# One clip instruction per attention step on VectorE, fed by four score matmuls in a row on TensorE, and a one-matmul output bias

## The reference

```
scores = einsum('bhnd,bhjcd->bhnjc', q, kc) / sqrt(Dh)
scores = clip(scores, -10.0, 10.0)
scores = where(mask == 0, -10.0, scores)
attn = softmax(scores, axis=-1)                 # over the 128 keys of one chunk
ctx = einsum('bhnjc,bhjcd->bhnd', attn, vc)
out = layernorm(ctx @ Wo.T + bo + x_normed) * gamma + beta
```

## Time and profile before

| | |
|---|---|
| median of 3 runs | 833.86 us (832.61 to 836.44) |
| profiled execution | 836.42 us, span 834.6 us, mean granted PE clock 0.904 |
| PE busy | 700.5 us, 84% |
| DVE busy | 727.4 us, 87% |
| ACT busy | 567.0 us, 68% |
| POOL busy | 556.9 us, 67% |
| chain that ended last | PE 43%, DVE 31%, POOL 12%, issue 10% |
| first clip to end of last clip | 38.58 to 513.39 us |

### The profile page before, as it was taken

The page is one execution under the profiler, slowest core; times in us unless marked ns, Lnnn a source line. Parts: engine busy times, 40 slices in busy tenths (PEclk is TensorE's granted clock), DMA queues, the critical chain, the costliest instruction groups (busy, mean ns, idle before and its releaser), DMA issues.

```text
span 834.6 us, 20579 instructions
## 1 busy us (share of the span) xinstructions
PE 700.5 (84%) x6443; PEld 366.1 (44%) x6443; DVE 727.4 (87%) x2032; ACT 567.0 (68%) x1091; POOL 556.9 (67%) x570
## 2 busy tenths in 40 slices
PE   4598699999999999999999898575620499999994
PEld 1322133333323233233333123464510499999994
DVE  4989999999999999999999999987661288888883
ACT  4596587897897987978978666534500377777772
POOL 1211557897887897987978999868777155555554
PEclk9789899999999999999999999555555599999998
DMA  8924503204105005013032001201111222222210
GB/s 281 241 56 118 130 2 88 66 1 126 28 26 127 2 27 126 3 55 98 1 102 52 1 2 38 65 27 30 40 53 53 54 66 71 80 76 77 66 49 2
DMA packets 47597, 54.37 MB, mean 65 GB/s; under 512 B 7668, under 2 KB 31313, under 8 KB 47490
## 3 DMA queue, kind: packets, MB, share of 16 engines
q10 hardware_dynamic: 12672, 23.07, 10.7%
q1 hardware_dynamic: 29858, 21.41, 9.6%
q0 software_dynamic: 4960, 8.58, 3.2%
HBM read 34.03 MB, written 20.75 MB: 66 GB/s over the span
## 4 chain that ended last, share of the span: by engine, by line
PE 43%; DVE 31%; POOL 12%; issue 10%; DMA 1%; ACT 1%; SPq 0%; POOLq 0%; DVEq 0%; ACTq 0%
PE score_ps L1494 8%; DVE rspread L999 7%; PE sum_ps L1508 7%; PE side_ps L1524 6%; POOL rows_dram L595 6%; DVE w L978 6%; DVE prob_ring L978 6%; PE score_ps L1452 3%; PE score_ps L1453 3%; PE score_ps L1454 3%; PE sum_ps L1734 2%; PE sum_ps L1740 2%; PE sum_ps L1736 2%; PE sum_ps L1738 2%; DVE prob_ring L988 2%
## 5 line engine op out<-in xcount | busy, mean ns | idle before, releaser
L1494 PE MATMUL score_ps<-stack_mem 128*128 128x512 f16 x512 | 158.3, 392 | 19.0 <-DVE prob_ring L978 13.4
L749 ACT ACTIVATE prob_ring<-prob_ring 128x1024 f32<-128x1024 f32 x128 | 134.2, 1054 | 49.3 <-DVE prob_ring L978 38.6
L535 POOL TENSOR_TENSOR ctx_sb<-ctx_sb,rspread 128x512 f32<-128x512 f32 x108 | 139.0, 1287 | 41.5 <-DVE rspread L999 32.5
L749 ACT ACTIVATE w<-w 128x1024 f32<-128x1024 f32 x128 | 134.2, 1055 | 33.1 <-DVE w L978 32.4
L978 DVE SCALAR_TENSOR_TENSOR w<-score_ps,limit 128x1024 f32<-128x1024 f32 x128 | 153.0, 1212 | 3.4 <-PE score_ps L1494 3.2
L978 DVE SCALAR_TENSOR_TENSOR prob_ring<-score_ps,limit 128x1024 f32<-128x1024 f32 x128 | 153.4, 1203 | 1.0 <-PE score_ps L1494 0.7
L602 POOL DMA_INDIRECT out_x<-xn,limit x91 | 89.7, 985 | 86.8 <-DVE xn L1349 71.1
L540 POOL TENSOR_TENSOR ctx_acc<-ctx_acc,ctx_sb 128x512 f32<-128x512 f32 x93 | 119.2, 1281 | 7.3
L1494 PEld LDWEIGHTS score_ps<-stack_mem 128*128 128x128 f16 x512 | 29.3, 97 | 183.0 <-issue 82.0
L872 ACT ACTIVATE xn<-score_ps,vec 128x128 f32<-128x128 f32 x364 | 99.1, 383 | 11.4 <-PE score_ps L1454 10.3
L999 DVE STREAM_SHUFFLE rspread<-prob_ring 128x256 f32<-128x256 f32 x256 | 101.5, 449 | 0.0
(11 more groups left out here) (236 smaller groups left out, 1591.1 us busy)
## 6 DMA issues: line engine op xcount, KB each, us to landing
stack_mem<-qk_dram ACTq DMA_DIRECT2D x56, 256.0 KB, 4.6
ctx_sb<-rows_dram SPq DMA_DIRECT2D x91, 66.5 KB, 1.9
qk_dram<-qk_hi ACTq DMA_DIRECT2D x16, 256.0 KB, 2.9
qk_dram<-qk_lo ACTq DMA_DIRECT2D x16, 256.0 KB, 4.1
x<-in_adj SPq DMA_DIRECT2D x4, 512.0 KB, 7.5
ctx_sb<-in_adj SPq DMA_DIRECT2D x4, 512.0 KB, 10.0
stack_mem<-qk_dram SPq DMA_DIRECT2D x16, 128.0 KB, 3.7
w<-in_L_ffn_W SPq DMA_DIRECT2D x4, 512.0 KB
```

The costliest lines, as they stand in the source:

```text
L535: pool.tensor_tensor(fresh, fresh, by, ALU.mult).then_inc(scaled_ready, 1)
L749: act.activation(prob_at(s, u), prob_at(s, u), ACT.Exp, scale=1.0 / SCORE).then_inc(exp_done, 1)
L1494: ins = pe.matmul(score_ps[:, h, :], kstack[:, par, h, k * P:k * P + P], qstack[:, par, h, half * HALF:half * HALF + HALF], start=True, st ...
```

## The change

- `clip` has no `u` any more. It is one instruction over all four heads, 128 x 2048, waits for all four scores of its step, and raises `clip_done` by 2.
- For that, the four probability buffers `w_mem` become slices of one tensor `w_all`, so that four heads lie side by side. `exp`, `contexts` and `denominators` keep their shapes and addresses.
- PE issues `scores(s + 1, 0)` and `scores(s + 1, 1)` together at the head of the step. `score_ps` is what it was.
- The bias parts lie on partitions 0 and 32 of a zeroed 128-row tile, and `wo` adds both in one matmul. Preparing it takes one more small DVE instruction and one more POOL memset, and the first sum is made on 64 partitions instead of one.

```
+        def probs_at(s):
+            r, of = s % 4 % 2, (w_all, prob_ring)[s % 4 // 2]
+            return of[:, HEADS * HALF * r:HEADS * HALF * (r + 1)].rearrange("p (h n) -> p h n", h=HEADS)
...
-            def clip(b, s, u):
-                dve.wait_ge(qk_done, 2 * STEPS * b + 2 * s + u + 1)
-                if u == 0:
-                    wait(dve, ctx_done, STEPS * b + s - 3)
-                    wait(dve, den_added, STEPS * b + s - 3)
+            def clip(b, s):
+                dve.wait_ge(qk_done, 2 * STEPS * b + 2 * s + 2)
+                wait(dve, ctx_done, STEPS * b + s - 3)
+                wait(dve, den_added, STEPS * b + s - 3)
                 k, half = s % T, s // T
                 dve.scalar_tensor_tensor(
-                    out=prob_at(s, u), in0=score_ps[:, 2 * u:2 * u + 2, :], scalar=-LIMIT * SCORE,
-                    in1=limit[:, k:k + 1, half * HALF:half * HALF + HALF].to_broadcast([P, 2, HALF]),
-                    op0=ALU.max, op1=ALU.min).then_inc(clip_done, 1)
+                    out=probs_at(s), in0=score_ps[:, :, :], scalar=-LIMIT * SCORE,
+                    in1=limit[:, k:k + 1, half * HALF:half * HALF + HALF].to_broadcast([P, HEADS, HALF]),
+                    op0=ALU.max, op1=ALU.min).then_inc(clip_done, 2)
...
-                    clip(b, s, 0)
+                    clip(b, s)
...
-                    clip(b, s, 1)
...
             def wo(n):
-                for i in range(2):
-                    pe.matmul(side_tiles(0), ones_row[0:1, :], bo_parts[:, i:i + 1, :].to_broadcast([1, TH, P]),
-                              start=(i == 0), stop=False)
+                pe.matmul(side_tiles(0), ones_row[:], bo_parts[:, :].rearrange("p (o d) -> p o d", o=1).to_broadcast([P, TH, P]),
+                          start=True, stop=False)
...
                 for s in range(STEPS):
                     next_scores(s, 0)
+                    next_scores(s, 1)
...
                     if STEPS * b + s - DEPTH + 1 in STARTS:
                         old_denominators(s)
-                        next_scores(s, 1)
                         old_contexts(s)
                     else:
                         old_contexts(s)
-                        next_scores(s, 1)
                         old_denominators(s)
```

More of the change, by code:

```diff
@@ L95, in gnn_moe @@
         qk_bias = sb("qk_bias", [P, 2], F32)
-        bo_parts = sb("bo_parts", [1, 2, P], F16)
-        bo_sum = sb("bo_sum", [1, P], F32)
-        ones_row = sb("ones_row", [1, P], F16)
+        bo_parts = sb("bo_parts", [P, P], F16)
+        bo_high = sb("bo_high", [64, P], F16)
+        bo_sum = sb("bo_sum", [64, P], F32)
+        ones_row = sb("ones_row", [P, P], F16)
         unscale = sb("unscale", [P, P], F16)
@@ L126, in gnn_moe @@
         gather_last = sb("gather_last", [P, TAIL, DH + 1], F32)
-        w_mem = [sb(f"w{1 + i // KH}_{i % KH}", [P, E * P], F32) for i in range(2 * KH)]
+        w_all = sb("w_all", [P, 2 * KH * E * P], F32)
+        w_mem = [w_all[:, E * P * i:E * P * (i + 1)] for i in range(2 * KH)]
         prob_ring = sb("prob_ring", [P, 2 * HEADS * HALF + HALF // 2], F32)
@@ L488, in _ @@
             pool.memset(neg_half[:], -0.5).then_inc(rstd2_ready, 1)
-            pool.memset(ones_row[:], 1.0).then_inc(bo_step, 1)
+            pool.memset(ones_row[:], 1.0)
+            pool.memset(bo_parts[:], 0.0).then_inc(bo_step, 1)
             pool.memset(unscale[:], 0.0).then_inc(consts_ready, 1)
@@ L1046, in _ @@
             dve.wait_ge(bo_done, 1)
-            dve.tensor_tensor(bo_sum[:], sum_ps[0:1, 0, 0:P], rows_bc[0:1, 0, :], ALU.add).then_inc(bo_step, 1)
+            dve.tensor_tensor(bo_sum[:], sum_ps[0:64, 0, 0:P], rows_bc[0:64, 0, :], ALU.add).then_inc(bo_step, 1)
             dve.wait_ge(bo_step, 2)
-            dve.tensor_copy(bo_parts[:, 0, :], bo_sum[:]).then_inc(bo_step, 1)
+            dve.tensor_copy(bo_high[:], bo_sum[:]).then_inc(bo_step, 1)
             dve.wait_ge(bo_step, 3)
-            dve.tensor_tensor(bo_parts[:, 1, :], bo_sum[:], bo_parts[:, 0, :], ALU.subtract).then_inc(bo_step, 1)
+            dve.tensor_copy(bo_parts[0:1, :], bo_high[0:1, :])
+            dve.tensor_tensor(bo_parts[32:33, :], bo_sum[32:33, :], bo_high[32:33, :], ALU.subtract).then_inc(bo_step, 1)
             copy_consts()
@@ L1551, in _ @@
                 v_proj(0, c, c)
-            pe.matmul(sum_ps[0:1, 0, 0:P], bv_total[:], woT[:], start=True, stop=True).then_inc(bo_done, 1)
+            pe.matmul(sum_ps[0:64, 0, 0:P], bv_total[:].to_broadcast([P, 64]), woT[:], start=True, stop=True).then_inc(bo_done, 1)
             pe.wait_ge(mask_made, T)
```

## The result

The changed kernel takes 856.72 us (median of 4 runs, 853.98 to 857.37). The kernel before took 834.17 us beside it (4 runs, 832.61 to 836.44). The ratio is 1.0259, with a 95% interval of 1.0241 to 1.0278: 22.5 us slower. The profiled execution's span is 854.8 us against 834.6, 20.2 more.

The account below looks back on a forecast made before the run. DVE and PE were both taken as full in the attention, with a scores-clip ring to bound short steps; 8.8 + 6.9 + 1.5 + 0.5 + 0.2 = +17.9 on 836.42 gave 854.3 profiled, 851 us as median, range 842 to 861.

Parts of the forecast that it names:

- Ring: Each step: clip 2.27, to scores 0.06, four scores 1.03, to clip 0.04; 3.40 us, the least a step takes.
- Steps 2 and 10: Middle-batch steps with the reciprocal: DVE's 2.87 plus 1.60 sets them, 4.47 us each.
- Steps 3 to 9, 12 and 14: Middle-batch steps with other work: 3 and 4 3.47 us, 5 to 8 and 12 3.57, 9 and 14 4.40.
- A middle batch: Sixteen steps of batches 1 to 6: 59.53 us against 58.06, +1.47 each and +8.8 for six.
- Batch 0: First batch, scores at half clock: three first steps of 4.23 us give +5.6, step 15 +1.3; +6.9 in all.
- Last batch and tail: Last batch: some six one-spread steps lose 0.45 each, +1.5 us; behind it ACT's later exponentials, +0.5.
- the clock rival: PE's clock falls once a batch from waits in steps; 1.3 to 2.6 us a batch more, 862 to 872, 4%.
- PE's sum: PE's work in a short step: scores 0.97, contexts 1.00, denominators 1.00; 2.97 us, perhaps 2.87.
- The bias: Output projection: one matmul fewer saves PE 0.22 us 16 times, 3.5, covered by DVE, nothing of the span.
- Preparation: Ahead of the first clip: one more DVE instruction, 0.1 to 0.3 us, entered as +0.2.
- Scores hidden behind DVE's work: Attention: DVE's work between clips covers the rest of the ring; batch 56.8 us, total 824, chance 4%.
- A clip of 2.17 or 2.42: Each step's clip cheap at 2.17 us, total 843, 9%; or saving nothing at 2.42, 868, 9% together with slower scores.

Follow-up runs that it names:

- experiment 3: The changed kernel with the old order on PE, contexts between the two pairs of scores: 1014.66 us, ratio 1.2161.
- experiment 5: The changed kernel with one score matmul made twice in each step, five in the row: 903.06 us on a second chip, ratio 1.0496.
- experiment 1: The changed kernel with the wide clip raising its semaphore by 1 instead of 2, readers counting steps: 854.06 us, ratio 1.024.
- experiment 6: The changed kernel with the old output bias of two one-row matmuls: 882.5 us on a second chip, ratio 1.0266.
- experiment 8: The changed kernel with its one bias matmul issued twice over all 128 rows: 885.23 us on a third chip, ratio 1.0262.
- experiment 4: The kernel before with the one-matmul output bias alone: 831.61 us, ratio 0.9975.
- experiment 2: The kernel before with both pairs of scores at the head of the step, clips left narrow: 857.25 us, ratio 1.0267.

## Why the prediction was right, point by point, and where it was short

The forecast of 851 us, range 842 to 861, held: 856.7. Its mechanism is shown by experiments 3 and 5. It stood 4.6 us below the measured loss on medians (17.9 against 22.5). In the attention it was 5.0 short (17.2 against 22.2): 3.8 in batches 1 to 6, 0.4 in batch 0 and 0.8 in the last; the 0.7 that it gave to the preparation and the tail did not show. The terms, in the order of the sum:

- **Ring, forecast 3.40, measured 3.48.** Clip 2.28 or 2.29 (2.27), clip to scores 0.06 (0.06), four scores 1.04 (1.03), scores to clip 0.09 (0.04). The mis-sized term is the last: the row it was read from had a clip that carries its wait. Experiment 1 gives 0.06 a ring step, 0.27 a batch. For the clip itself the Trainium skill's estimate of 2.26 ("VectorE: DVE Perf Modes", "The TRN2 errata") was within 0.03 of the trace.
- **Steps 2 and 10, forecast 4.47, measured 4.69 and 4.68.** This was the largest error in a batch, 0.43. The forecast took the reciprocal's price from a start-to-start distance with a clip behind it, 1.66. Now the shuffle stands behind it, which reads its result: it starts 1.80 after the reciprocal's start (238.38 to 240.18), 0.04 or 0.05 after its end, where the clip had started 0.08 before the end. The other part is 0.06 that I had taken off for a short clip. What makes the difference is the semaphore: the shuffle waits for `rinv_ready`, which the reciprocal raises. The trace has one other pair of this kind, `post_res` and `post_stats` (a tensor add and the statistics that wait for it, L1014 and L1022), and there too the second starts 0.03 after the first one's end, in both kernels; a shuffle, a clip or a `qk_low` that doesn't wait for its neighbour in front starts some 0.08 before that one's end. So this term could have been read before the change, from `post_stats`.
- **Steps 3 to 9, 12 and 14** came out at 3.48 to 3.55, 4.40, 3.50 and 4.42 against 3.47 to 3.57, 4.40, 3.57 and 4.40: right. **Step 15** took 3.54 for 3.40. There the next batch's scores started 0.15 after the clip's end instead of 0.06; they also wait for `stacked`, which may be why, but no run shows it.
- **A middle batch, forecast 59.53, measured 60.25.** Over the five batches from 2 to 6 that is 3.6 us, most of what was missing.
- **Batch 0, forecast +6.9, measured +7.3.** Its slow first steps took 4.38, 4.44 and 4.37 for 4.23, step 15 took 4.39. In this timeline of DVE and PE the scores run at 1.2 GHz (1.89 for a row of four, forecast 1.86):

```profile
37.02 2.29 DVE L984 SCALAR_TENSOR_TENSOR w_all<-score_ps,limit 128x2048 f32<-128x2048 f32 x1 [1.13 <-PE score_ps L1500]
41.40 2.29 DVE L984 SCALAR_TENSOR_TENSOR w_all<-score_ps,limit 128x2048 f32<-128x2048 f32 x1 [2.08 <-PE score_ps L1500]
```

```profile
39.37 1.89 PE L1500 MATMUL score_ps<-stack_mem 128*128 128x512 f16 x4 [2.48 <-DVE w_all L984]
```

- **Last batch and tail, forecast +2.0, measured +2.3 and -0.46.** One step, number 7, took 4.31 for 3.40: PE had stood still for 1.94 us and its scores then ran at 1.2 GHz. That is the clock rival in one place, but the change is not what brought it. The kernel before had scores at 1.2 GHz in the same batch, behind a pause of 0.88, and the prediction overlooked them when it wrote that only the standstill of 5.73 us brought the clock down. And in experiments 1, 3, 5, 6 and 8 the same pause of 1.94 us was followed by scores at the full clock. The two rows are from the kernel before and from the changed one:

```profile
480.39 1.04 PE L1494 MATMUL score_ps<-stack_mem 128*128 128x512 f16 x2 [0.88 <-DVE prob_ring L978]
```

```profile
500.57 1.89 PE L1500 MATMUL score_ps<-stack_mem 128*128 128x512 f16 x4 [1.94 <-DVE prob_ring L984]
```

- **The clock elsewhere.** The granted clock is 1.00 in the middle batches, 2.4 GHz, with pauses of 0.58 us in most steps. The page of the Trainium skill that the prediction cites ("TensorE: Matmul & The Clock Gate", "A second HAM failure mode") tells of a kernel whose clock swung with small pauses between groups of matmuls; these pauses did not make it swing.
- **PE's sum, forecast 2.97 or 2.87 for a short step, measured 2.83.** From the rows above, scores 0.96 and contexts 0.89; denominators take 0.98 where the next scores follow them at once. I had put the saving down to neighbours that are both fp32. The rows say otherwise. Behind the scores (fp16, 128*128) the fp32 transposes (128*128) start after 0.87 us, as the fp16 bias matmul (128*128) does in experiment 8, and the contexts (fp32, 128*32) after 0.96. The tenth comes between fp32 groups of different shape too: in the records the four fp32 transposes start 0.11 us apart, and the contexts 0.20 behind the last of them (239.40 to 239.93 in all). So the tenth belongs to the change of the tile's shape, not of the type; experiment 8 shows it for one-row matmuls, these rows of the timeline for groups 32 columns wide.
- **The bias, "3.5 us of PE and nothing of the span".** Nothing of the span holds (experiment 6). PE's part was mis-sized, 16 x 0.52 = 8.3 us by experiments 6 and 8. And the cover belongs to the changed kernel: without the ring the same edit brings 2.4 us (experiment 4), within the "up to 3.5" that the prediction gave for it.
- **Preparation, forecast +0.2, measured -1.56 in this pair of profiles.** This is most likely no effect of the edits. The instruction `bo_sum` ahead of the first clip starts at 34.3 to 34.7 us in eight of the ten profiles, and at 37.6 and 37.8 in two, the kernel before and experiment 2. Ahead of it stand VectorE instructions that make the bf16 mask out of the int32 adjacency. In the two late profiles one of the last four took 3.41 us instead of 0.69. A POOL addition of 128 x 1024 began beside these four in all ten; it took 2.25 and 2.42 us in the two, and 3.1 to 3.9 in the other eight. The kernel before, then the changed one:

```profile
24.04 5.28 DVE L1041 TENSOR_SCALAR w<-ctx_sb 128x1024 bf16<-128x1024 int32 x4
```

```profile
23.73 2.49 DVE L1047 TENSOR_SCALAR w_all<-ctx_sb 128x1024 bf16<-128x1024 int32 x4
```

So it was now DVE and now POOL that was held up, and the attention waits for DVE. Both late profiles are of kernels with the old bias and the old buffers, and no run tells that apart from chance. But had the kernel before always been late, experiment 4 would have gained some 5 us, its 2.6 in the attention and 2.6 more ahead of it, and it gained 2.4. It also fits that the profiled execution of the kernel before lay 2.6 above its median.
- **Signs.** DVE's busy time was to be under 57.5 in each batch and was 57.73 in the middle ones. The idle time ahead of the clips was to be released by PE's scores in some six steps, and is: six steps of batch 3 have 0.19 to 0.50, under the name "issue".
- **Rivals.** Scores hidden behind DVE's work: false, DVE idles 2.5 us a batch. A clip of 2.17 or 2.42: 2.28. The clock: one step beyond batch 0 and the head of batch 1, and there, as in these two, it had run low before as well.

## What to carry to other kernels

Before fusing instructions into one, ask which buffer they share and how many copies of it there are: two half-size clips let two engines alternate on one set of PSUM banks, and the single one ties them into a ring of 3.48 us where each had under 3 us of work. (A second `score_ps` beside the wide clip was not tried.) Add up that ring and compare it with each engine's own sum, step by step, for idle time in one step isn't won back in the next. Moving work in one engine's queue can close another loop, as in experiment 2, so look for what the moved instruction stands in front of. And an edit worth nothing in one kernel (the bias) may be worth 2.4 us in its neighbour, so try such edits apart.

## What the runs showed of the hardware

- A VectorE instruction that raised its semaphore by 2 had its wait in a separate instruction ahead, and started 0.09 us after PE's last score; raised by 1 it carried the wait and started after 0.04 (experiment 1). The profile then names the releaser instead of "issue".
- A change of a matmul group's tile shape cost PE 0.10 us on going from 128*128 to 128*32 or to 1*128, and 0.2 on the way back from 1*128 (0.09 ahead of the first matmul, 0.10 behind it); a change of type at the same shape cost nothing. A bias through one-row matmuls cost 0.52 us a step more than one through a single matmul of 128 rows, though it has only one matmul more, of 0.22.
- On VectorE an instruction that did not wait for the one in front started some 0.08 us before that one's end; one that waited for its semaphore started 0.03 to 0.05 after it (shuffle behind reciprocal, statistics behind an addition).
- Four VectorE conversions from int32 to bf16 and one POOL addition at the same time held each other up: either a conversion took 3.41 us for 0.69, or the addition 3.1 to 3.9 for some 2.3. That they hold up each other is read from the ten profiles; no run took one of them away.
- The same pause of PE, 1.94 us, was followed by scores at 1.2 GHz in one profile and at 2.4 GHz in five.
- On one chip the stages behind the attention took 321 us, on two others 348 and 351 us with the same code there, while short steps of the attention took 3.48 us on all three.
